# Wider slot rings, one transfer for edge and destination columns, and the softplus logarithm in PSUM, in a two-layer graph kernel

## What is computed

```python
def _cgconv(x, src, dst, edge_attr, Wf, bf, Ws, bs, gamma, beta, rmean, rvar):
    z = jnp.concatenate([x[dst], x[src], edge_attr], axis=-1)
    msg = jax.nn.sigmoid(z @ Wf + bf) * jax.nn.softplus(z @ Ws + bs)
    n = x.shape[0]
    summed = jax.ops.segment_sum(msg, dst, num_segments=n)
    cnt = jax.ops.segment_sum(jnp.ones((dst.shape[0],), x.dtype), dst, num_segments=n)
    out = summed / jnp.maximum(cnt, 1.0)[:, None]
    out = (out - rmean) * jax.lax.rsqrt(rvar + BN_EPS) * gamma + beta
    return out + x
...
x = _layernorm(x + _L0_gnn_ref(x, edge_index, edge_attr_64, ...), axis=-1)
```

## Time and profile before

| | us |
|---|---|
| median of 3 runs | 2270.21 (2269.26 to 2273.01) |
| the profiled execution | 2270.27 |
| its span, first to last instruction | 2268.5 |
| mean granted TensorE clock | 0.798 of full speed |

### The profile page before, as it was taken

How to read it: one execution, slowest core, us unless ns; L and a number is a source line. 1 busy time by engine, 2 the same in 40 slices (tenths; PEclk the granted TensorE clock), 3 DMA queues, 4 the chain that set the end, 5 groups by cost and what they waited for, 6 DMA issues and landing times. The chain is left out here.

```text
span 2268.5 us, 35513 instructions
## 1 busy us (share of the span) xinstructions
PE 1578.1 (70%) x7507; PEld 1356.8 (60%) x7507; DVE 1660.3 (73%) x3577; ACT 1382.3 (61%) x1690; POOL 1609.7 (71%) x1587
## 2 busy tenths in 40 slices
PE   7567766776777767677577777666677676767773
PEld 6456665665666666566456666655566565656662
DVE  3677777777777777777557777777777776777777
ACT  4466666666666666666426666666666665666664
POOL 3477777777777777777336777777777777777770
PEclk9888888778778787788698777888787877887775
DMA  8676666666666566666486666666665656666652
GB/s 280 206 193 174 173 176 177 171 177 175 174 181 174 170 179 176 172 177 178 122 280 179 184 177 173 176 179 171 174 177 171 181 174 174 182 176 175 176 155 65
DMA packets 266858, 402.90 MB, mean 178 GB/s; under 512 B 81121, under 2 KB 164270, under 8 KB 266671
## 3 DMA queue, kind: packets, MB, share of 16 engines
q0 software_dynamic: 75264, 205.62, 32.8%
q1 hardware_dynamic: 190974, 194.77, 28.9%
q10 hardware_dynamic: 434, 0.81, 0.1%
HBM read 370.94 MB, written 30.04 MB: 177 GB/s over the span
## 5 line engine op out<-in xcount | busy, mean ns | idle before, releaser
L328 POOL DMA_INDIRECT pre<-s_rows,ends x1568 | 1590.4, 1014 | 569.8 <-issue 442.9
L368 PE MATMUL pre_ps<-rhs,lhs 128*128 128x256 f32 x3136 | 1047.2, 492 | 615.3 <-DVE lhs L553 584.8
L368 PEld LDWEIGHTS pre_ps<-rhs,lhs 128*128 128x128 f32 x3136 | 727.7, 243 | 776.7 <-DVE lhs L553 481.8
L568 DVE TENSOR_TENSOR pre<-pre_ps,pre 128x1024 f32<-128x1024 f32 x392 | 479.3, 1223 | 334.1 <-DMA pre<-s_rows,ends 328.9
L426 ACT ACTIVATE pre<-pre 128x512 f32<-128x512 f32 x392 | 247.0, 630 | 778.0 <-DVE pre L568 773.5
L378 PEld LDWEIGHTS sum_ps<-hot,msg 128*128 128x128 f32 x3136 | 526.6, 230 | 52.8 <-DVE msg L580 11.4
L378 PE MATMUL sum_ps<-hot,msg 128*128 128x64 f32 x3136 | 492.3, 305 | 12.2 <-DVE msg L580 12.2
L431 ACT ACTIVATE logs<-pre 128x1024 f32<-128x1024 f32 x392 | 414.4, 1057 | 12.4
L437 ACT ACTIVATE logs<-logs 128x1024 f32<-128x1024 f32 x392 | 414.1, 1056 | 12.4
L553 DVE TENSOR_SCALAR lhs<-dst_b,base_f,part 64x256 f32<-64x256 f32 x784 | 302.2, 430 | 96.2 <-issue 57.4
L573 DVE SCALAR_TENSOR_TENSOR logs<-pre,logs 128x512 f32<-128x512 f32 x392 | 268.6, 685 | 1.7 <-ACT logs L437 1.7
(11 more groups left out here) (58 smaller groups left out, 181.4 us busy)
## 6 DMA issues: line engine op xcount, KB each, us to landing
dst_b<-dst_floats SPq DMA_DIRECT2D x392, 128.0 KB
lhs<-edge_cols SPq DMA_DIRECT2D x392, 128.0 KB
rhs<-d_rows SPq DMA_DIRECT2D x784, 64.0 KB
pre<-s_rows,ends POOLq DMA_INDIRECT x1568, 3.2
s_rows<-pre SPq DMA_DIRECT2D x24, 512.0 KB, 4.2
d_rows<-logs SPq DMA_DIRECT2D x24, 512.0 KB, 5.9
out<-y_out SPq DMA_DIRECT2D x12, 256.0 KB, 2.3
sp_tab<-group_table SPq DMA_DIRECT2D x100, 0.0 KB
```

The source lines that it names most:

```text
L328: nc.gpsimd.indirect_dma_start(pre[:, j, i, 0:F2], None, s_dram, bass.IndirectOffsetOnAxis(ap=ends[:, k, j * TILES + i, 0:1], axis=0)).the ...
L368: ins = nc.tensor.matmul(pre_ps[:, j % 2, i, :], lhs[:, j, i * P:(i + 1) * P], rhs[:, j, i // 2, :], start=True, stop=True)
L568: nc.vector.tensor_tensor(pre[:, j, :, 0:F2], pre_ps[:, j % 2], pre[:, j, :, 0:F2], ALU.add).then_inc(s_pre[j], 1)
```

## The change

- Ring sizes: `pre`, `lhs`, `rhs` have `RING = 7` slots, one a step in turn (`slot`), where they had four. `logs` has two, and a new PSUM buffer `soft_ps` has two. `dst_b` is gone.
- One DMA a step loads edge columns (64 rows) and destinations (64 equal rows of integers) together, prepared on the host as `edge_cols` in DRAM. The compare reads the integers from the lower half of `lhs` and writes the one-hot there. The table of float destinations in DRAM is gone.
- The logarithm is two instructions: the gate's half stays in `logs`, softplus's half goes to `soft_ps`; softplus reads and writes it there, the message reads it there.
- The windows' positions are read from `base_i`; `wins` and its load are gone.
- Stages for the tables: seven buffers for s, five for d (in `logs`, `msg`, `hot`).
- Ends of the first three groups, the first three bases and the edge columns of four steps are loaded ahead of the loop. The plan's tables are stored by POOL, ahead of its two memsets; node weights come in pieces, the biases and edge weights are loaded by ScalarE's queue, ScalarE's root comes behind its copies, the flag's matmul at the 13th tile.
- Layer 2's update of x_t moves from the d tiles into the first 25 steps.

```diff
+EARLY = 3
+RING = 7
-        lhs = sb("lhs", [P, SLOTS, STEP], F32)
-        dst_b = sb("dst_b", [P, SLOTS, STEP], F32)
-        rhs = sb("rhs", [P, SLOTS, PAIRS, F2], F32)
-        pre = sb("pre", [P, SLOTS, TILES, 3 * F], F32)
-        logs = sb("logs", [P, SLOTS, TILES, F2], F32)
+        lhs = sb("lhs", [P, RING, STEP], F32)
+        rhs = sb("rhs", [P, RING, PAIRS, F2], F32)
+        pre = sb("pre", [P, RING, TILES, 3 * F], F32)
+        logs = sb("logs", [P, 2, TILES, F2], F32)
+        soft_ps = ps("soft_ps", [P, 2, TILES, F], F32)
+        s_stage = [pre[:, r, :, 0:F2] for r in range(RING)]
+        d_stage = [logs[:, 0], logs[:, 1], rows_of(msg[:, 0:2]), rows_of(msg[:, 2:4]), rows_of(hot[:])]
...
+        def slot(k, j):
+            return (SLOTS * k + j) % RING
+        def loaded(eng, sems, b, k, j, each_inc):
+            eng.wait_ge(sems[slot(k, j)], b * (SLOTS * each_inc) + ((SLOTS * k + j) // RING + 1) * each_inc)
...
+            def load_edges(at, edge):
+                sp.dma_start(lhs[:, at, :], d["edge_cols"][:, bass.ds(edge, STEP)]).then_inc(edge_in[at], 16)
+            for k in range(EARLY):
+                load_ends(k, k)
+            for c in range(8):
+                sp.wait_ge(s_copied, 2 * c + 2)
+                store_rows(sp, s_dram, s_stage, c, s_out)
+            if first:
+                sp.wait_ge(table_out, 48)
+            bodies = n_bodies(sp)
+            at = sp.value_load(t["choice"][:, 1:2], min_val=0, max_val=GENERAL_AT * ROW)
+            load_table(at)
+            for k in range(EARLY):
+                load_base(at + k * ROW, k)
+            for c in range(8, STORES):
+                sp.wait_ge(s_copied, min(2 * c + 2, DOUBLES))
+                store_rows(sp, s_dram, s_stage, c, s_out)
+            for n in range(SLOTS):
+                load_edges(n, n * STEP)
+            for c in range(STORES):
+                sp.wait_ge(d_added, min(2 * c + 2, DOUBLES))
+                store_rows(sp, d_dram, d_stage, c, d_out)
+            for r in range(len(d_stage)):
+                sp.wait_ge(d_out[r], 16 * len(range(r, STORES, len(d_stage))))
...
-                    done(sp, s_hot_t, g, j, SLOTS)
+                    done(sp, s_prod, g, j, RING)
                     sp.sem_inc(passed, 1)
-                    sp.dma_start(dst_b[WIN:P, j, :], t["dst_dram"][bass.ds(blk * GROUP + j * STEP, STEP)]
-                                 .rearrange("(a c) -> a c", a=1).to_broadcast([WIN, STEP])).then_inc(dst_in[j], 16)
-                    done(sp, s_prod, g, j, SLOTS)
-                    sp.sem_inc(passed, 1)
-                    sp.dma_start(lhs[0:FE, j, :], d["edge_t"][:, bass.ds(blk * GROUP + j * STEP, STEP)]
-                                 ).then_inc(edge_in[j], 16)
-                    for q in range(PAIRS):
-                        sp.dma_start(rhs[FE:P, j, q, :], d_dram[bass.ds(bases[PAIRS * j + q], WIN), :]
-                                     ).then_inc(d_in[j], 16)
+                    if not (isinstance(g, int) and g == 0):
+                        load_edges(slot(k, j), blk * GROUP + j * STEP)
+                    load_rows(slot(k, j), j, bases)
...
-                    done(pool, s_soft, g, j, SLOTS)
+                    done(pool, s_soft, g, j, RING)
...
+            act.dma_start(rhs[0:FE, :, :, :].rearrange("p s k f -> p (s k) f"),
+                          d[f"w_edge{layer}"].unsqueeze(1).to_broadcast([FE, RING * PAIRS, F2])).then_inc(rhs_in, 16)
             if first:
+                act.wait_ge(eps_added, 1)
+                nc.scalar.activation(root[:], bn[:, :, 3], ACT.Sqrt).then_inc(rooted, 1)
...
-                done(act, s_msg, g, j, SLOTS)
+                done(act, s_msg, g, j, 2)
...
-                nc.scalar.activation(logs[:, j], logs[:, j], ACT.Ln, bias=1.0).then_inc(s_logs[j], 1)
+                nc.scalar.activation(logs[:, j % 2, :, 0:F], logs[:, j % 2, :, 0:F], ACT.Ln, bias=1.0).then_inc(s_log_f[j], 1)
+                done(act, s_msg, g, j, 2)
+                nc.scalar.activation(soft_ps[:, j % 2], logs[:, j % 2, :, F:F2], ACT.Ln, bias=1.0).then_inc(s_log_s[j], 1)
...
+                if first and i == 3:
+                    v.wait_ge(rooted, 1)
...
-                    ins = nc.vector.tensor_scalar(lhs[WIN:P, j, cols], dst_b[WIN:P, j, cols],
+                    ins = nc.vector.tensor_scalar(lhs[WIN:P, at, cols], lhs[WIN:P, at, cols].bitcast(I32),
...
-                nc.vector.scalar_tensor_tensor(logs[:, j, :, F:F2], pre[:, j, :, F:F2], 0.0, logs[:, j, :, F:F2],
+                nc.vector.scalar_tensor_tensor(soft_ps[:, j % 2], pre[:, at, :, F:F2], 0.0, soft_ps[:, j % 2],
                                                ALU.max, ALU.add).then_inc(s_soft[j], 1)
...
-                nc.vector.tensor_tensor(msg[:, j], logs[:, j, :, F:F2], logs[:, j, :, 0:F], ALU.mult
+                nc.vector.tensor_tensor(msg[:, j], soft_ps[:, j % 2], logs[:, j % 2, :, 0:F], ALU.mult
...
+                step = SLOTS * k + j
+                if not first and isinstance(b, int) and live(0) and step < DOUBLES:
+                    cols = slice(step * F2, (step + 1) * F2)
+                    nc.vector.scalar_tensor_tensor(t["x_t"][:, cols], t["x1_t"][:, cols], t["bn_shift"][:, 1:2],
+                                                   t["x_t"][:, cols], ALU.add, ALU.add)
...
-                    v.wait_ge(wins_in, g * 16)
-                    v.sem_inc(passed, 1)
-                    sum_at = load_bases()
-                    v.sem_inc(dve_has, 1)
+                    sum_at = load_bases((k - 1) % BODY)
```

## The result

The changed kernel takes 2149.87 us (median of 4 runs, 2149.06 to 2152.32) against 2271.61 us (4 runs, 2269.26 to 2276.36) before, on the same chip: ratio 0.9463, 95% interval 0.9445 to 0.9481, 121.7 us less. The forecast was 2155.6 us.

The account below looks back on a forecast made before the run. POOL, issuing gathers without rest, was taken as the bound. Loops 70.8, layer 1's start 26.1 and layer 2's 19.3, less 1.5, gave 114.7 us off 2270.27: 2155.6 us, range 2120 to 2180, chance 0.70.

Parts of the forecast that it names:

- the loops: Steady gathers of both layers: 755 after each restart, 0.0478 and 0.0460 us shorter in period, 70.8 us gained.
- the two restarts: POOL's resumption after its stop at each layer's start: 9.2 us earlier in layer 1, 3.5 in layer 2.
- the rest: Small losses: 1.0 us for gathers beside layer 2's moved x update, 0.5 us for the tails, 1.5 in all.
- Part 1: Softplus's logarithm in PSUM: gathers no longer lengthened by softplus and message, 0.048 us less excess a gather.
- 1.2536 + 0.020: New gather period in the loops: a gather alone plus the unchanged compare and one-hot share, 1.274 us.
- Part 2: Seven slots: 28 gathers instead of 16 before each stop, 15.9 us a layer, plus a 1.0 us wait gone in layer 1.
- stores at 379 GB/s: Layer 1's start: 11 MB at this rate take 29 us, so POOL starts near 34 us.
- Part 3: Restart after the last d store: chain 1.4 us shorter and that store earlier; restarts at 78.3 and 1198.2 us.
- Part 4: Remaining edits: vanished issues and integer compare gain nothing, moved x update loses 1.0 us, tails 0.5 us.
- (c): Rival: the in-place integer compare runs at 6.1 ns an element, making VectorE decide: 2655 us, chance 0.04.
- (b): Rival: VectorE and PE become the bound in the loops at 5.2 us a step, losing 38: 2194 us, chance 0.12.
- (a): Rival: a PSUM destination or one SBUF input still holds GpSimd up, so the excess stays: 2226 us, chance 0.10.

Follow-up runs that it names:

- a1: The changed kernel with softplus's logarithm in SBUF again, where softplus and message read and write it: 2890.32 us, ratio 0.9889.
- a4: The changed kernel with softplus's logarithm in SBUF but softplus's result in PSUM, where the message reads it: 2880.0 us, ratio 0.9851.
- a2: The kernel before with only the PSUM logarithm added, softplus and message using it there: 2958.22 us, ratio 1.0109.
- e2: The kernel of e1 with softplus's logarithm in SBUF, so softplus and message read two SBUF operands: 4187.23 us.
- e1: The changed kernel with a ring of four and each gather issued twice, first into a spare tile nobody reads: 4117.23 us.
- c1: The same kernel as a1, run on another chip: 2878.15 us, ratio 0.9895.
- c4: The changed kernel with one scalar operand in the compare and SP's first-group register reads ahead of the d stores: 2870.99 us, ratio 0.9876.
- d runs: The changed kernel unaltered, 2832.58 us (0.9865), and without the two additions of window sums to node sums in each step, 2875.11 us (1.0002).

## Why the prediction was right

**The sum.** 114.7 us were forecast and 121.1 measured, and this is closer than its parts: the loops gave 10.3 us more, the two restarts 5.0 less, the rest 1.1 more. That much of the agreement is luck.

**What bounds.** Right: POOL alone, before and after, waiting for its own issuing, with VectorE waiting for gathers (79.1 / 119 = 0.66 us a step, 0.78 before).

**Part 1.** The mechanism is shown by four kernels (`a1`, `a4`, `a2`, and `e2` against `e1`), the price by the last pair: 0.18 to 0.20 us a step, forecast 4 x 0.047 = 0.19. Softplus's and the message's share of the excess in the loops was 73.6 us before and is 0.2 after, which is the 70.8 of the forecast. The gain of the loops was 10 us larger all the same: 82.1 us against 70.8 and 1.0. The step that failed is the sum 1.2536 + 0.020 for the period: a gather alone takes 1.2510 (47.80 to 61.56, 11 gathers) and what compare and one-hot leave is (13.9 + 7.5) / 1420 = 0.015 where 0.020 was taken over unchanged; the measured periods are 1.2652 and 1.2683. The phase of these instructions against the gathers shifted, which the range allowed for. By all starts in the loops, compare and one-hot leave 11.3 us in layer 1 and 13.0 in layer 2 (before: 16.7 and 14.3), and layer 2's moved update of x_t 0.7, where 1.0 was forecast. A gather alone took 0.948 us in the execution before and 0.946 in this one (0.945 in `a1`, 0.948 in `c1`: it changes from one execution to another), and the pauses between gathers are 0.001 us shorter; the two count for some 5 us. The Trainium skill (SBUF — State Buffer, Who interferes with whom) was right that two SBUF inputs contend with a GpSimd instruction that reads SBUF. Its inference that descriptor generation escapes a two-input instruction doesn't hold for these gathers, by the 200 of 200 in `e2`. But they also read their row numbers from SBUF (`ends`), so the section's first rule may cover them; which part of a gather is held up, no run separates.

**Part 2.** 28 gathers at each start, as forecast, and 15.9 and 15.8 us. Its times weren't: POOL starts at 42.68, not near 34. The step that failed is "stores at 379 GB/s": before the ninth s store SP reads two registers and issues four small loads (stores pause between 22.7 and 27.4 us, and 25 to 30 moves 75 GB/s). The last s store was issued at 30.7 and landed at 40.35, beside edge columns and the first d stores, and 2.3 us more passed until the first gather, with a register read of POOL's own between. It cost nothing, since the 28th gather (76.72) still comes before the restart; POOL's rest of 1.80, less the usual 0.30, left 1.5 us.

**Part 3.** The restart of layer 1 was forecast at 78.3 and came at 79.47, by two errors of opposite sign. The last d store was over at 64.2 (forecast 65.5). That it was so close is luck in part: the DMA engines had moved 21.9 MB by then, a mean of 341 GB/s with the pause of part 2 in it, where the forecast had 23.4 MB at 370. The chain behind it took 15.3 us and not 12.8: 2.1 us between that wait and the table's issue, 1.84 of it one register read of SP, and 0.55 to the first rows of d. In the kernel before that read was done ahead of the d stores; I took the chain's two vanished issues off and missed the read that moves in. In layer 2 the same step takes 2.7 us and ate the gain (restart 15.8 behind the landing of the last d store, 13.9 before, where the forecast took 1.4 off), so 3.5 became -0.3. `c4` shows it from the other side: with the read early, 2.3 us come back in layer 1, and in layer 2 POOL rests 22.05 us before the restart where it rests 23.84 in `c1`.

**Part 4 and the rivals.** Two compares with integer input take 0.79 us a step (309.0 / 392), and took 0.77 with float input (302.2 / 392), so (c) falls by its row. (b) falls since POOL never waits in the loops on this chip; its margin was 0.66 us a step of VectorE. On the chips of the d runs a relative of (b) holds: the loop of VectorE and TensorE is the bound, by late signals rather than by work, and the change is worth 1.35% instead of 5.4%. (a) falls by `a4` and by the counts.

## What to carry to other kernels

Where GpSimd's gathers set the pace, look at what VectorE is doing when each gather starts: an instruction with two SBUF inputs stretches it until 0.12 us before its own end, and moving one input to PSUM takes that away at no cost to VectorE (0.69 and 0.68 us as before). When code is taken out of a start-up chain, list what the new order puts in, register reads by the issuing engine above all. And before a gain is promised for other chips, see that the same engine is the bound there.

## What was not expected of the hardware

- ScalarE's logarithm L453 of 128x512 takes 583 ns with its result in PSUM and 612 ns with it in SBUF (`a1`; 392 of each). L451, to SBUF in both, takes 629.
- A gather is held up to 0.12 us before the end of the VectorE instruction, and only if that one began first. The one-hot does it too (59 of 59), and so does the compare with its single tensor input (141 of 156), but not to gathers that start in its first 0.10 us (0 of 24).
- On three of the chips of these runs TensorE's signals reach the other engines some 3 us behind the shown end of the matmul and bunched, but almost only while GpSimd gathers, and the same kernel takes 2833 us instead of 2150.
